# Shared expert in five chunks of 128 inner columns and a joined one, its outputs added to memory as whole rows

## The reference

```python
# x: [3072, 512]; 64 experts, 6 for each row, at most 64 rows for each expert; inner width 352
g = jnp.einsum('ech,ehi->eci', buf, w_gate)
u = jnp.einsum('ech,ehi->eci', buf, w_up)
y = jnp.einsum('eci,eih->ech', jax.nn.silu(g) * u, w_down)
...
# the shared expert sees all rows; inner width IS = 704
shared = jax.nn.silu(x @ sw_gate) * (x @ sw_up) @ sw_down
return y + shared
```

## Time and profile before

| | us |
|---|---|
| median of 3 runs | 1470.52 (1469.61 to 1470.71) |
| profiled execution, its own time | 1472.85 |
| its span from first to last instruction | 1471.1 |
| TensorE busy in the span | 1248.9 |
| VectorE, ScalarE, GpSimd busy | 757.1, 419.8, 498.9 |

### The profile page before, as it was taken

How to read it: one execution, slowest core, us unless ns; L and a number is a source line. 1 busy time by engine, 2 the same in 40 slices (tenths; PEclk the granted TensorE clock), 3 DMA queues, 4 the chain that set the end, 5 groups by cost and what they waited for, 6 DMA issues and landing times. The chain is left out here.

```text
span 1471.1 us, 23499 instructions
## 1 busy us (share of the span) xinstructions
PE 1248.9 (85%) x9192; PEld 795.6 (54%) x9192; DVE 757.1 (51%) x1667; ACT 419.8 (29%) x695; POOL 498.9 (34%) x453
## 2 busy tenths in 40 slices
PE   5263778889898999999987879999999999969995
PEld 5252443445454454646444868666666666646662
DVE  7993566666776867786854352232233222312321
ACT  2221214444444443535354421111111111111110
POOL 0000101111213434343466374334444434343444
PEclk9597779999999999999999899999999999989998
DMA  3033231312425151524271484799999999888993
GB/s 113 1 75 85 53 72 42 84 42 71 122 60 133 36 136 22 151 42 127 45 230 43 133 277 61 221 312 298 309 327 343 302 329 349 264 259 298 332 284 41
DMA packets 141109, 239.82 MB, mean 163 GB/s; under 512 B 61368, under 2 KB 81480, under 8 KB 141000
## 3 DMA queue, kind: packets, MB, share of 16 engines
q1 hardware_dynamic: 117160, 214.10, 45.8%
q0 software_dynamic: 23840, 24.23, 9.2%
HBM read 175.59 MB, written 38.90 MB: 146 GB/s over the span
## 5 line engine op out<-in xcount | busy, mean ns | idle before, releaser
L1993 POOL DMA_INDIRECT out_rows<-mo_y,mo_scatter_half x128 | 180.9, 1413 | 253.9 <-DMA out_rows<-mo_y,mo_scatter_half 183.7
L1355 DVE TENSOR_REDUCE at_maxes<-at_ps 128x1 f32<-128x384 f32 x384 | 195.3, 552 | 63.3 <-PE at_ps L916 56.6
L1122 ACT ACTIVATE bulk<-at_ps 128x1152 f32<-128x1152 f32 x128 | 144.6, 1129 | 272.2 <-PE at_ps L883 250.5
L1616 POOL DMA_INDIRECT slot_table<-at_toki,at_si x144 | 143.6, 997 | 105.7 <-DVE at_maxes L1355 74.0
L70 PE MATMUL mo_ps<-arena_view,arena_view 128*117 128x384 f32 (+1 forms) x864 | 168.8, 344 | 1.1 <-PEq L570 1.1
L70 PEld LDWEIGHTS mo_ps<-arena_view,arena_view 128*117 128x117 f32 (+1 forms) x864 | 146.5, 179 | 14.6 <-issue 14.5
L916 PE MATMUL at_ps<-late_view,late_view 128*128 128x384 bf16 x384 | 117.0, 355 | 35.9 <-DVE at_maxes L1355 18.1
L874 PE MATMUL at_ps<-arena_view,arena_view 128*128 128x512 f32 (+1 forms) x576 | 115.6, 352 | 3.8 <-ACT arena_view L1209 2.3
L874 PEld LDWEIGHTS at_ps<-arena_view,arena_view 128*128 128x128 f32 x576 | 90.7, 193 | 36.9 <-issue 22.4
L916 PEld LDWEIGHTS at_ps<-late_view,late_view 128*128 128x128 bf16 x384 | 31.2, 98 | 145.4 <-DVE at_maxes L1355 108.5
L883 PE MATMUL at_ps<-arena_view 97*128 97x384 f32 x384 | 97.8, 364 | 9.6 <-DMA arena_view<-at_mrow 5.1
(11 more groups left out here) (222 smaller groups left out, 1774.4 us busy)
## 6 DMA issues: line engine op xcount, KB each, us to landing
bulk<-in_L_ffn_w_gate SPq DMA_DIRECT2D x32, 704.0 KB
bulk<-in_L_ffn_w_up SPq DMA_DIRECT2D x32, 704.0 KB
late_view<-in_L_ffn_w_gate SPq DMA_DIRECT2D x32, 704.0 KB
late_view<-in_L_ffn_w_up SPq DMA_DIRECT2D x32, 704.0 KB
arena_view<-arena_view SPq DMA_DIRECT2D x96, 192.0 KB
late_view<-in_L_ffn_w_down SPq DMA_DIRECT2D x32, 512.0 KB
bulk<-in_L_ffn_w_down SPq DMA_DIRECT2D x32, 512.0 KB
out_rows<-at_hr SPq DMA_DIRECT2D x8, 768.0 KB, 3.8
```

Of the source, the lines that this page charges most:

```text
L1122: A.activation(PT[:, N % RING, :, :], ps[:, 0:NT, 0:SEQ], ACT.Exp, scale=float(HD) ** -0.5)\
L1355: V.tensor_reduce(maxes[:, half, s, h:h + 1], ps[:, raw_bank(a, u), 0:SEQ], AX.X, ALU.max, negate=True)\
L1616: G.indirect_dma_start(slot_table, bass.IndirectOffsetOnAxis(ap=si[:, e % 2, m:m + 1], axis=0), toki[:, e % 2, m // TOPK:m // TOPK + 1], N ...
L1993: G.indirect_dma_start(acc_halves, bass.IndirectOffsetOnAxis(ap=scatter_half[:, half, 2 * p + e:2 * p + e + 1], axis=0), y[:, p % 2, e, co ...
```

## The change

The 704 columns become five chunks of 128 and a rest of 64 (`SW = [128]*5 + [64]`, `SC` stays 6). For the rest, gate and up are one unit: the weights are laid out so that its 64 gate columns and 64 up columns stand side by side, and one block of 12 matmuls makes both (gate in PSUM partitions 0 to 63, up in 64 to 127). Its hi part is kept in partitions 64 to 127 and its lo part in 0 to 63 of the same tile, with the down weights stored twice (both halves of the partitions), so an out unit takes 5 times 3 plus 2 = 17 matmuls. A sequence has 11 + 3 = 14 units. The load of the up weights is cut in two DMAs, and the rest's down weights are loaded twice. Behind the joined unit ScalarE does Silu and then the hi copy, and VectorE the multiplication between them. The shared expert's add is one DMA of 384 whole rows of 512 columns on a semaphore of its own, `shared_added`; it waits for both halves of all pairs ahead of it, and each pair's add waits for both its half and `shared_added`.

```diff
-SHARED_UNITS = 15
+SHARED_UNITS = 14
...
-        self.gu_raw = part(arena, 0, [2, 2, self.KC, IS])
-        self.gu = part(arena, 0, [2, 2, self.KC, IS], F32R)
+        self.GU = 2 * self.SC - 1
+        self.lower, self.upper = slice(0, P // 2), slice(P // 2, P)
...
+    def is_rest(self, c):
+        return c == self.SC - 1
+
+    def gate(self, c):
+        return self.lower if self.is_rest(c) else slice(0, P)
+
+    def hidden(self, c):
+        return self.upper if self.is_rest(c) else slice(0, P)
+
+    def low(self, c):
+        return (self.lower, 0) if self.is_rest(c) else (slice(0, P), 1)
 
     def into_hidden(self, T, out, c, g):
         last = 3 * self.KC - 1
         for n in range(last + 1):
             k, (xa, wa) = n // 3, ((0, 0), (0, 1), (1, 0))[n % 3]
-            m = T.matmul(out, self.gu[:, wa, g, k, self.SO[c]:self.SO[c] + self.SW[c]], self.x2[:, xa, k, :],
-                         start=(n == 0), stop=(n == last))
+            first = self.SO[c] + (self.SO[-1] + P if g else 0)
+            cols = slice(first, first + P)
+            m = T.matmul(out, self.gu[:, wa, k, cols], self.x2[:, xa, k, :], start=(n == 0), stop=(n == last))
         return m
 
     def out_of_hidden(self, T, out, s):
-        last = 3 * self.SC - 1
-        for n in range(last + 1):
-            c, (xa, wa) = n // 3, ((0, 0), (0, 1), (1, 0))[n % 3]
-            m = T.matmul(out, self.h[0:self.SW[c], xa, c, s * P:(s + 1) * P], self.d[0:self.SW[c], wa, c, :],
-                         start=(n == 0), stop=(n == last))
+        steps = [(c, xa, wa) for c in range(self.SC - 1) for xa, wa in ((0, 0), (0, 1), (1, 0))]
+        steps += [(self.SC - 1, 0, wa) for wa in range(2)]
+        for n, (c, xa, wa) in enumerate(steps):
+            m = T.matmul(out, self.h[:, xa, c, s * P:(s + 1) * P], self.d[:, wa, c, :],
+                         start=(n == 0), stop=(n == len(steps) - 1))
         return m
...
-                for g, w in enumerate((sw_gate, sw_up)):
-                    sp.dma_start(shared.gu_raw[:, 1, g], w.rearrange("(k p) i -> p k i", p=P)).then_inc(w_staged[g], 16)
+                IS, rest = shared.IS, shared.SO[-1]
+                for g, w, place, cols in ((0, sw_gate, 0, slice(0, IS)), (1, sw_up, rest + P, slice(0, rest)),
+                                          (1, sw_up, IS, slice(rest, IS))):
+                    sp.dma_start(shared.gu_raw[:, 1, :, place:place + cols.stop - cols.start],
...
-                sp.dma_start(shared.d_raw[0:SW[c], 1, c, :], sw_down[shared.SO[c]:shared.SO[c] + SW[c], :])\
-                    .then_inc(w_staged[2], 16)
+                for half in ((shared.lower, shared.upper) if shared.is_rest(c) else (slice(0, P),)):
+                    sp.dma_start(shared.d_raw[half, 1, c, :], sw_down[shared.SO[c]:shared.SO[c] + SW[c], :])\
+                        .then_inc(w_staged[2], 16)
...
             def mult_shared(i, c):
-                n = SC * i + c
+                n, rows, rest = SC * i + c, shared.hidden(c), shared.is_rest(c)
                 dve.wait_ge(s_silu_done, n + 1)
-                dve.wait_ge(s_up_done, n + 1)
+                if rest:
+                    dve.wait_ge(s_gate_done, n + 1)
+                else:
+                    dve.wait_ge(s_up_done, (SC - 1) * i + c + 1)
                 wait(dve, s_hi_done, n - 1)
-                V.tensor_tensor(shared.sh[0:SW[c], c % 2, :], shared.sil[0:SW[c], :],
-                                ps[0:SW[c], gate_bank(i, c) + 1, 0:SEQ], ALU.mult).then_inc(s_mult_done, 1)
+                V.tensor_tensor(shared.sh[rows, c % 2, :], shared.sil[rows, :],
+                                ps[rows, gate_bank(i, c) + (0 if rest else 1), 0:SEQ], ALU.mult).then_inc(s_mult_done, 1)
 
...
-    SC = (IS + P - 1) // P
-    SW = [IS // SC + (1 if c < IS % SC else 0) for c in range(SC)]
+    SC = IS // P + 1
+    SW = [P] * (SC - 1) + [IS % P]
+    assert 2 * SW[-1] == P
...
-    rank = {add: EARLY - 1 + n for n, add in enumerate(order)}
+    pairs_ahead = {add: sum(a[0] == "pair" for a in order[:n]) for n, add in enumerate(order)}
+    shared_ahead = {add: EARLY - 1 + n - pairs_ahead[add] for n, add in enumerate(order)}
...
-                if step < 2 * SC and g == 1:
+                if step < shared.GU and (g == 1 or shared.is_rest(c)):
...
             def out_shared(u):
                 i, step = sequence(u)
-                s = step - 2 * SC
+                s = step - shared.GU
                 dve.wait_ge(s_down_done, NT * (i - EARLY) + s + 1)
-                for half in added:
-                    dve.wait_ge(half, 16 * (rank["shared", i - 1] + 1))
+                dve.wait_ge(shared_added, 16 * (shared_ahead["shared", i - 1] + 1))
                 V.tensor_copy(shared.so[:, s, :], ps[:, out_bank(s), :]).then_inc(so_ready, 1)
...
-                        wait(pool, added[half], 16 * rank["pair", p, e])
+                        wait(pool, added[half], 16 * pairs_ahead["pair", p, e])
+                        wait(pool, shared_added, 16 * shared_ahead["pair", p, e])
...
             def add_shared(i):
                 wait(pool, so_ready, NT * (i - EARLY + 1))
                 for half in range(2):
-                    cols = slice(half * D // 2, (half + 1) * D // 2)
-                    wait(pool, added[half], 16 * rank["shared", i])
-                    G.dma_start(acc[i * SEQ:(i + 1) * SEQ, cols].rearrange("(s p) d -> p s d", p=P),
-                                shared.so[:, :, cols], accum_op=ALU.add).then_inc(added[half], 16)
+                    wait(pool, added[half], 16 * pairs_ahead["shared", i])
+                wait(pool, shared_added, 16 * shared_ahead["shared", i])
+                G.dma_start(acc[i * SEQ:(i + 1) * SEQ, :].rearrange("(s p) d -> p s d", p=P),
+                            shared.so[:], accum_op=ALU.add).then_inc(shared_added, 16)
```

More of the change, by code:

```diff
@@ L1794, in shared_unit @@
                 before = NT * (i - EARLY - 1)
-                if step < 2 * SC:
+                if step < shared.GU:
                     c, g = divmod(step, 2)
@@ L1897, in _ @@
                 for half in added:
-                    wait(act, half, 16 * (rank["pair", p - 2, 0] + 1) if p >= 2 else 0)
+                    wait(act, half, 16 * (pairs_ahead["pair", p - 2, 0] + 1) if p >= 2 else 0)
                 A.activation(y[:, p % 2, 0, :], ps[0:CAP, 4, :], ACT.Copy).then_inc(ya_ready, 1)
@@ L1946, in after_unit @@
                     lo_shared(u)
-                if step >= 2 * SC:
+                if step >= shared.GU:
                     out_shared(u)
-                if step == 2 * SC + 1 and i + 1 < NSEQ:
+                if step == shared.GU + 1 and i + 1 < NSEQ:
                     split_x2(i + 1)
@@ L1979, in _ @@
                 for half in added:
-                    wait(dve, half, 16 * (rank["pair", p - 2, 1] + 1) if p >= 2 else 0)
+                    wait(dve, half, 16 * (pairs_ahead["pair", p - 2, 1] + 1) if p >= 2 else 0)
                 V.tensor_copy(y[:, j, 1, :], ps[CAP:P, 4, :]).then_inc(yb_ready, 1)
```

88 lines of the change are left out of this document (50 added, 38 removed).

## The result

The change makes the kernel slower: 1493.9 us (median of four runs, 1490.42 to 1495.93) against 1470.62 (four runs, 1469.61 to 1488.12), a ratio of 1.0156 with an interval of 1.0115 to 1.0198. The forecast was 1462 us, its range 1449 to 1472. The profiled execution has a span of 1488.6 us, 17.6 more than before.

A forecast was written before the change was run, and what follows sets the result against it. TensorE was taken to set the pace, with the chain of adds nearly as long. Experts' phase -8.9, attention's end -3.0 and hole +3.9 sum to -8.0: 1472.85 profiled gives 1464.8, less 2.3 for the median 1462 us; range 1449 to 1472.

The forecast's parts named there:

- TensorE's term: Experts' phase on TensorE: fewer hidden units and out matmuls, less longer waits behind the joined unit; -8.9 us.
- Hidden and out units: Experts' phase: six hidden units fewer save 6.8 us; eighteen out units, one matmul less each, save 4.2 us.
- the wait behind the joined unit: Experts' phase: Silu first lengthens the first out unit's wait by 0.55 us in three pairs, 1.65 us in all.
- the free loads of 128 columns: Hidden units' matmuls: weight loads widened from 117 to 128 columns stay hidden and cost nothing.
- the last rival: Wider weight loads show: 9 ns on every hidden-unit matmul, 0.11 us per unit, sum +0.3, 1471 us; chance 0.03.
- The attention's end: End of attention, before the experts' phase: fewer unit matmuls less one more DMA issue; -3.0 us, bounds -4.6 and -0.4.
- The landing: Whole-row shared add, from issue to the next pair's first half: 11.0 us, bounds 8.8 and 13.8.
- The hole, measured at VectorE, grows by 5.1 us: Wait before pair 23's G: 4.4 + 1.5 - 4 x 0.2; a unit covers 1.2, leaving +3.9 us.
- a gain of 0.2 us for each add: Chain of adds: next pair's second half goes at 13.6 us against 13.8 before; between 2.4 and -2.6.
- The chain eats it all: Rival: the hole at pair 23 grows by 9 to 14 us, time 1468 to 1473; chance 0.15.
- Slower: Rival: whole-row add lands no sooner than both halves did; hole term +16.8 us, time 1475; chance 0.12.
- The hole closes: Rival: whole-row add frees the chain by 4 us or more, pair 23's loss goes; 1447 to 1450 us; chance 0.23.

The follow-up runs named there:

- halves: Kernel before with only the new chunks; shared adds stay two column halves on the semaphores of the pairs' adds: 1469.09 us, ratio 1.0042 to the kernel before.
- joined: Changed kernel with its shared add cut into two DMAs of 256 columns, both still waiting for both chains: 1491.25 us, ratio 1.0143 to the kernel before.
- hold: Changed kernel with one pair's gate and up weights held back until the shared add of sequences 2 to 6 landed: 1477.72 us, ratio 1.0113 to kernel before.

## Why the prediction was wrong

**TensorE's term was right.** Hidden and out units, the wait behind the joined unit and the free loads of 128 columns made -8.9; without the adds it is 505.43 less 496.54, 8.9. That the two agree to 0.1 us is luck, with one execution on each side; the ratios give 8.2 us for this term and the attention's end together, where the terms say 11.9, with an interval of some 7 us either way. The units of 12 with weights of 128 columns take 2.36 behind T (1116.29 above) and 2.33 to 2.38 elsewhere. That is over the 2.33 which I had named as a sign of being wrong, but by 0.03 and not by the 0.11 of the last rival, which is out.

**The attention's end** was put at -3.0, bounds -4.6 and -0.4. The first T is 4.2 earlier. The mean over the ten profiled kernels with the new chunks is 919.8, over the four with the old 924.1: 4.3 less, with a scatter of 13 us in the first group. The number fits, but by luck: two of its parts are wrong, and the errors cancel. The first is SyncE's issuing of the down weights, which I had priced at +1.15 us for one DMA more. With the change it is

```profile
799.98 4.40 SPq L856 DMA_DIRECT2D arena_view<-in_L_ffn_sw_down  x7
805.74 1.01 SPq L757 DMA_DIRECT2D at_hr<-tokens_h  x2
806.80 1.57 SPq L759 DMA_DIRECT2D at_hr<-in_txt  x1
```

and before, behind the six of rows 12, it was

```profile
807.29 7.38 SPq L741 DMA_DIRECT2D at_hr<-tokens_h  x2
814.72 3.41 SPq L743 DMA_DIRECT2D at_hr<-in_txt  x1
```

Seven DMAs of 128 and 64 rows are issued in less time than six of 118 and 117, and the last residual's rows are issued 8 us sooner. It is so in all fourteen profiled kernels: 4.4 us in the ten with the new chunks, 6.8 to 6.9 in the four with the old. VectorE's last addition for the residual now ends at 819.5, where it ended at 823.1. These 3.6 us are most of why the first group of out units starts 4.6 us earlier:

```profile
818.81 0.69 DVE L1409 TENSOR_TENSOR at_hr<-at_hr,at_ps 128x512 f32<-128x512 f32 x1 [3.10 <-PE at_ps L894]
...
861.81 13.72 PE L93 MATMUL at_ps<-arena_view,arena_view 128*128 128x512 f32 x51 [7.18 <-DVE arena_view L1477]
```

From the end of the residual to this group it is 42.3 us where it was 43.4 (42.4 and 43.0 in the mean over the ten and the four), so the unit saved ahead of it gave about what I took, 0.9. The second wrong part is what lies behind. From this group to the first T I had counted 3.2 us less. It is 60.96 us now and was 60.55. Over all kernels it is 57.7 to 66.2 with the new chunks and 59.7 to 64.0 with the old, so what is saved there is not shown.

**The landing was mis-sized by little in the mean.** I took 11.0 us from the issue to the next pair's first half; the four adds of sequences 2 to 5 took 10.6, 14.3, 8.6 and 14.8, 12.1 in the mean. By my own rate of 4 us for 1 us of landing that is 4 us of time, and the forecast was 32 short. The single ones lie outside the bounds of 8.8 and 13.8 at both ends, and the lower bound had been misread: sequence 3's halves took 7.7 us before. For the second half I had 13.6 from where the first of the old adds would have gone, and the four took 12.4, 16.1, 10.4 and 16.6 from their issue, 13.9, as long as before (13.8).

**The step that failed** is the one that turns late adds into time: "The hole, measured at VectorE, grows by 5.1 us". It added four mean landings up to pair 22's copy, as if a late add counted only there. That hole grew by 4.2 us (11.4 to 15.6), nearly as forecast. What the sum put at nothing was every other place: 10.8 us at the copy of pair 11, 12.2 at that of pair 27, where before no result copy had waited for adds, and 7.8 in smaller waits. Each add stands before a margin of its own. The chunks alone broke through these two, by TensorE's lead and by where the weights' loads then fell (6.4 and 8.5 us of wait at the same copies in halves), and the joined add, with landings of 14.3 and 15.4 us, made it 10.8 and 12.2. Under it lies "a gain of 0.2 us for each add". It priced a joined add by the second half of the next pair alone, as if the first column had nothing to lose. With the same chunks the join costs 14.8 us (joined against halves). At the add of sequence 3 the first column goes 11.8 us later than before; 5.2 of these lie ahead of the add, which I had put at 0.9.

**A cost that the sum lacked.** I charged the hole's slow matmuls at 1.3 us and only in the rival. With three holes and smaller waits it is 10 us over the stretch, at a granted clock of 0.97 against 1.00.

**The rivals.** What came is what the rivals "The chain eats it all" and "Slower" were about, both at once: the chunks' 8.9 us vanish in the chain already with the old adds (halves, 519.71 against 517.92), and the add makes it slower. "Slower" had the place right and gave 1475; it counted only the hole at pair 23 and from a landing of 13.0 us on, while 12.1 was enough. "The hole closes" would have needed single late adds; the buffers show that this is not so. Two slips in the prediction bear on the rivals only: the chance of 0.03 for the loads, with a time of 1471, was counted with "faster", which should have been 0.70; and the smaller waits for adds before, put at pairs 16 to 19, were at the copies of pairs 14, 17, 18 and 24. The kernels do not settle what share of each landing is the taking of turns with the weights: hold shows that it is at least some 6 us for the add of sequence 3, but the held weights then ran beside other adds.

## What to carry to other kernels

Two chains of dependent transfers that run apart hide each other's slow landings; a transfer that joins them for fewer DMAs gives this up, and can cost more than its landing says, here 14.8 us. Where a chain of transfers runs nearly as long as the engine that sets the pace, take the transfers out in a trial first: it shows at once what a saving on the engine is worth, here 8.9 us on TensorE that came to nothing. And when waits depend on margins, price each late transfer against its own margin, not their sum against one, and count what a quicker engine takes from each margin.

## What the runs showed that I had not expected

The time up to the experts' phase scatters: first T from 914.4 to 927.7 us in single profiled executions. The stretch from first to last T without adds had the length that was worked out for it to within 1 us in the kernel before (506 against 505.43), but was 12.5 us off in the changed one (509 against 496.54). A fourth buffer cut the waits for adds from 28.1 to 3.0 us and gave no time back. The DMAs of down weights by 128 and 64 rows were issued in 4.4 us where six by 118 and 117 rows had taken 6.9, and the three DMAs behind them went up to 8 us sooner. And each of the three long stalls of TensorE is followed by slower matmuls: G's 32 took 7.35, 7.07 and 6.78 us where 4.95 is usual, so that these holes cost 19 to 28% more than their wait (6.27, or 12%, at the one before).
